# A megakernel's last stage: a new order of its steps

## The chip, the cores and the metric

One core of a Trainium2 chip runs the whole program. The metric is the device time of one execution in microseconds. Three timed runs of the kernel before took 4629.72, 4630.22 and 4632.44 us; the median is 4630.22.

## What is computed

Four layers over 16 images of 128 channels and 32 x 32 pixels: attention with 8 heads, a whitening and colouring of the channels, a block with spatial gate, two attentions and a feed-forward part, and last an attention with one head. The changed stage computes what stands here, the end of the third layer and the fourth:

```python
# end of the third layer (its attentions are done; ff_w1's product is what the stage reads)
fused = jax.nn.silu(combined @ ff_w1.T + ff_b1) @ ff_w2.T + ff_b2
final = fused @ out_w.T + out_b
final = group_norm(final.transpose(0, 2, 1).reshape(b, c, h, w), post_g, post_b)
x = final + residual
# fourth layer: C8 = 16, N = 1024 pixels
q = jnp.einsum('oc,bcn->bno', Wq, xf) + bq
k = jnp.einsum('oc,bcn->bon', Wk, xf) + bk[None, :, None]
v = jnp.einsum('oc,bcn->bon', Wv, xf) + bv[None, :, None]
energy = jnp.einsum('bno,bom->bnm', q, k)
attention = jax.nn.softmax(energy, axis=-1)
out = jnp.einsum('bcm,bnm->bcn', v, attention).reshape(B, C, H, W)
return gamma[0] * out + x
```

## The kernel before

The program is a row of stages that follow one another, each with its own semaphores: `attend` for layer one, `statistics`, `whiten`, `gate`, `attend` again, and `closing`, which is the stage at hand. Nothing of `closing` overlaps the stage ahead of it. Its first transfers are issued at 4015 us of the span.

`closing_steps` (L1347) writes the order by hand: each step of each image gets a place on a line on which an image is 8 long and its eight score steps stand at 0.05, 1.05 and so on. The steps are sorted by place, and every engine walks the same sorted list and issues what of each step is its own, in that order, with waits on semaphores ahead of it. So a place says nothing of a time; only the order of an engine's own steps counts. The numbers of buffers come from the same list (`numbered`): each use of a bank waits until the use before it in that bank is read.

The steps of image b, in the order of their data:

- load (SP): both inputs, ff and h, 512 KB each.
- silu: ScalarE a tanh (L1629), VectorE u = (ff + bias) / 2 (L1702) and s = (tanh + 1) * u (L1707).
- w23: a 128 x 128 product in two halves on TensorE (L1563), ScalarE writes fin (L1634).
- stats, group, factors: the group norm. VectorE's statistics (L1053 to L1059), a small product (L1566), VectorE (L1066 to L1072), a power -0.5 on GpSimd (L1513), VectorE g_a and g_b (L1078 to L1083), and ScalarE hb = h + g_b (L1640).
- z: VectorE (L1723), fin * g_a + hb. z is the input of the attention.
- reach, bound, ratio, scales: a bound on the queries and keys, by which they are scaled into half precision (L1729 to L1731, L1569, L1737, L1738, L1516 to L1521, L1743 to L1747).
- qk: two halves of TensorE (L1572), which ScalarE scales (L1648).
- split: GpSimd writes two half-precision parts (L1526, L1528).
- stack (SP): 12 small transfers that put these parts under each other (L1478).
- pair (8 of them): TensorE's scores of 128 queries against 1024 keys (L1584), of which VectorE takes the maxima (L1761).
- lowest, turn: the maxima negated (L1766), transposed by TensorE (L1589), written by VectorE as two half-precision rows (L1771, L1773), and put into the stack by four transfers (L1483).
- score (8 of them, called 0.0 to 0.3 and 1.0 to 1.3 for the two halves of the queries): TensorE's product again, now transposed and with the maxima subtracted (L1596); ScalarE's exponentials (L1658).
- v: values in two halves (L1576), VectorE scales them (L1754).
- pv ("values" below): e times v, four instructions each (L1609), four steps into one bank, and evac: ScalarE's copy of that bank (L1663).
- esum: GpSimd adds the exponentials, three steps a half (L1537, L1540); dsum: TensorE sums them over partitions (L1616), VectorE copies (L1779); sums (SP), recip (VectorE, L1784), invstore and wide (SP): the inverse, spread over all partitions.
- norm: GpSimd osb * inverse (L1544); zb: ScalarE (L1668); final: VectorE's sum (L1790); store (SP, L1501).

TensorE, VectorE, ScalarE, GpSimd and SP thus work on several images at once. Two pairs of banks go round among group, bound, v, pair, turn and dsum: each of these steps needs the bank that the last but one of them used. Three single banks go round among w23, qk and score, and one is left for values. Of the exponentials there are eight buffers, an image's worth.

Of the kernel before, what the change touches and what calls it, by code (L numbers as in the profile page):

```python
# [19 lines left out]
KC = N // P  # L20
# [40 lines left out]
class Heads:  # L61
# [3 lines left out]
    def __init__(self, kind, n, first):  # L65
# [11 lines left out]
                load=-19.4, reach=-15.96, bound=-4.74, qk=(-3.04, -2.27, -0.19, 2.66), v=(1.75, 2.73), proj=(15.99, 17.54)),  # L77
    True: dict(score=0.01, values=0.12, evac=0.13, score2=0.14, rate=(1.79, 1.95, 1.41), lead=(5.35, 4.59, 7.74), lowest=0.17, turn=0.72,
               load=-26.48, reach=-44.42, bound=-21.92, qk=(-20.62, -17.56, 1.31, 1.34), v=(5.02, 12.31), dqk=(0.36, 4.41, 5.28, 9.56),
               dsum=11.93, proj=(25.58, 31.69), first=((-11.0, -3.0), (-3.0, 5.0), (5.0, 12.5), (12.5, 19.5), (19.5, 25.5)))}  # L80
# [1263 lines left out]
                                                   op0=ALU.add, op1=ALU.mult).then_inc(gated_ready, 1)  # L1344


def closing_steps():  # L1347


    at = []  # L1350
    add = lambda time, *step: at.append((time, len(at), step))
    SCORE, VALUES, PIECE, MAXIMA = 0.05, 0.2, 0.5, 0.8
    for b in range(NB):
        start = 8 * b
        add(start - 34, "load", b)
        add(start - 31, "silu", b)
        for half in range(2):
            add(start - 29 + half + PIECE, "w23", b, half)
            add(start - 18 + half + PIECE, "qk", b, half)
            add(start - 5 + half + PIECE, "v", b, half)  # L1360
        add(start - 27.1, "stats", b)
        add(start - 26 + PIECE + 0.01, "group", b)
        add(start - 24.9, "factors", b)
        add(start - 23.8, "z", b)
        add(start - 23, "reach", b)
        add(start - 22 + PIECE + 0.01, "bound", b)
        add(start - 21.4, "ratio", b)
        add(start - 20.0, "scales", b)
        add(start - 16.4, "split", b)
        add(start - 14.5, "stack", b)  # L1370
        for qc in range(KC):
            add(start - 11 + qc + MAXIMA, "pair", b, qc)
        add(start - 3.01, "lowest", b)
        add(start - 3 + MAXIMA + 0.05, "turn", b)
        for i in range(8):
            add(start + i + SCORE, "score", b, i // 4, i % 4)
            add(start + i + 2 + VALUES, "pv", b, i // 4, i % 4)
            if i % 4:
                add(start + i + 0.3, "esum", b, i // 4, i % 4)
        for half in range(2):  # L1380
            add(start + 4 * half + 6, "evac", b, half)
        add(start + 10 + PIECE, "dsum", b)
        add(start + 11, "sums", b)
        add(start + 12.3, "recip", b)
        add(start + 12.4, "invstore", b)
        add(start + 13.3, "wide", b)
        add(start + 14.9, "norm", b)
        add(start + 15.0, "zb", b)
        add(start + 16.1, "final", b)
        add(start + 16.2, "store", b)  # L1390
    return [step for _, _, step in sorted(at)]


def closing(nc, M, V, shared, half_b1, w23, b23, ff_in, h_in, out, scratch):


    zero, ident, ones = (shared[n] for n in ("zero", "ident", "ones"))
    steps = closing_steps()
    st_n = numbered(steps, w23=1, qk=1, score=2)
    mr_n = numbered(steps, group=1, bound=1, v=1, pair=1, turn=1, dsum=1)  # L1400
# [585 lines left out]
```

## Time and profile before

| | |
|---|---|
| median of three timed runs | 4630.22 us |
| the profiled execution's own time | 4632.01 us |
| its span | 4630.2 us |
| mean granted clock of TensorE | 0.955 |
| busy over the whole span: TensorE, VectorE, ScalarE, GpSimd | 89%, 78%, 67%, 33% |
| the last stage, from its first transfer to the end | 4015 to 4630 us |
| busy in one image of its steady part (34.2 us): TensorE, VectorE, ScalarE, GpSimd | 29.9, 26.8, 15.3, 22.8 us |

The page's busy shares are means over stages with different limits, so for this change only the last 615 us are read, image by image. A matmul's busy time is modelled and overlaps the next one's by some 0.07 us; VectorE's and ScalarE's lines overlap their next by about 0.1.

### The profile page before, as it was taken

What the parts mean: (1) busy time and instruction counts of PE and PEld (TensorE: products, weight loads), DVE (VectorE), ACT (ScalarE), POOL (GpSimd) and SP (SyncE); (2) the same over time, 40 slices, a digit from 0 to 9 for tenths busy, and PEclk for the clock granted to TensorE, in tenths of its full rate; (3) what the DMA queues carried; (4) which work ended last, traced back from release to release, by engine and by line L of the source; (5) the groups of instructions that cost most, each with busy time, mean ns of one, the idle gap of its engine ahead of it and who ended that gap; (6) DMA issues with size and microseconds to landing.
All of it is one profiled execution on the core that took longest, in us unless ns stands there. A gap on an engine that the chain in (4) does not pass through costs nothing. (4 is left out here: it accounts for less than half of the span.)

```text
span 4630.2 us, 68670 instructions
## 1 busy us (share of the span) xinstructions
PE 4126.7 (89%) x25550; PEld 1202.0 (26%) x25550; DVE 3594.3 (78%) x4166; ACT 3116.6 (67%) x5561; POOL 1536.1 (33%) x862
## 2 busy tenths in 40 slices
PE   5999999999996775799999999999999999578888
PEld 1222222222221732122222222222222222123333
DVE  7999999999993366788777777788777777278774
ACT  1888888888886454467777777777777777334443
POOL 1111111111110033144433344444433343346666
PEclk6999999999998987899999999999999999779999
DMA  2222322323321254111112212122122210112221
GB/s 62 55 53 63 67 49 65 66 47 67 65 43 45 73 191 139 35 39 46 38 38 49 47 43 50 38 45 49 33 44 50 46 35 18 46 55 73 71 70 53
DMA packets 144281, 261.96 MB, mean 57 GB/s; under 512 B 58192, under 2 KB 58192, under 8 KB 143824
## 3 DMA queue, kind: packets, MB, share of 16 engines
q1 hardware_dynamic: 143952, 257.61, 22.1%
q8 instruction: 201, 3.29, 0.3%
q14 instruction: 128, 1.05, 0.1%
HBM read 155.13 MB, written 85.13 MB: 52 GB/s over the span
## 5 line engine op out<-in xcount | busy, mean ns | idle before, releaser
L703 DVE TENSOR_REDUCE c_mx<-banks 128x2 f32<-128x1024 f32 x1280 | 1525.1, 1220 | 347.4 <-PE banks L496 192.0
L596 ACT ACTIVATE c_e<-banks 128x512 f32<-128x512 f32 x2560 | 1388.4, 595 | 595.7 <-PE banks L530 323.2
L703 DVE TENSOR_REDUCE a_mx<-banks 128x2 f32<-128x1024 f32 x1024 | 1208.9, 1219 | 62.8 <-PE banks L496 53.1
L596 ACT ACTIVATE a_e<-banks 128x512 f32<-128x512 f32 x2048 | 1111.1, 594 | 177.5 <-PE banks L520 155.5
L545 PE MATMUL banks<-a_e,a_vs 128*32 128x512 f32 x4096 | 545.5, 605 | 0.2 <-ACT a_e L596 0.2
L545 PE MATMUL banks<-c_e,c_vs 128*32 128x512 f32 x4096 | 545.5, 605 | 0.0
L441 POOL TENSOR_TENSOR c_esum<-c_e,c_esum 128x1024 f32<-128x1024 f32 x224 | 527.5, 2355 | 36.6 <-ACT c_e L596 11.2
L496 PE MATMUL banks<-a_stack 48*128 48x512 f16 x2048 | 391.4, 391 | 78.4 <-DMA a_stack<-k_halves 25.9
L520 PE MATMUL banks<-a_stack 50*128 50x512 f16 x2048 | 399.4, 387 | 48.2 <-ACT a_e L596 35.1
L520 PE MATMUL banks<-c_stack 50*128 50x512 f16 x2048 | 398.2, 385 | 45.6 <-ACT c_e L596 36.1
L496 PE MATMUL banks<-c_stack 48*128 48x512 f16 x2048 | 377.0, 387 | 23.4 <-DVE c_mx L703 16.9
L438 POOL TENSOR_TENSOR c_esum<-c_e,made 128x1024 f32<-128x1024 f32 x32 | 60.5, 1892 | 689.5 <-ACT c_e L596 689.5
L545 PE MATMUL banks<-c_e,c_vd 128*64 128x512 f32 x1024 | 275.9, 617 | 0.1
L406 POOL TENSOR_TENSOR a_parted<-a_reach,a_over 128x1 f32<-128x1 f32 x16 | 3.1, 191 | 821.8 <-DVE a_reach L685 821.8
L1609 PE MATMUL banks<-d_e,d_vd 128*128 128x512 f32 x512 | 271.2, 655 | 2.6 <-issue 1.9
L520 PEld LDWEIGHTS banks<-c_stack 50*128 50x128 f16 x2048 | 98.7, 93 | 582.8 <-ACT c_e L596 550.0
L520 PEld LDWEIGHTS banks<-a_stack 50*128 50x128 f16 x2048 | 99.3, 93 | 567.1 <-ACT a_e L596 544.3
L1658 ACT ACTIVATE d_e<-banks 128x512 f32<-128x512 f32 x256 | 137.8, 591 | 123.5 <-PE banks L1596 123.0
L526 PE MATMUL banks<-c_dparts 64*128 64x512 f16 x1536 | 208.3, 376 | 1.9 <-ACT c_e L596 1.9
L504 PE MATMUL banks<-c_dparts 64*128 64x512 f16 x1536 | 202.7, 376 | 1.9 <-DVE c_mx L703 1.8
L496 PEld LDWEIGHTS banks<-c_stack 48*128 48x128 f16 x2048 | 96.7, 94 | 408.2 <-DVE c_mx L703 258.1
L496 PEld LDWEIGHTS banks<-a_stack 48*128 48x128 f16 x2048 | 100.2, 94 | 331.5 <-DVE a_mx L703 238.3
(322 smaller groups left out, 4466.1 us busy)
## 6 DMA issues: line engine op xcount, KB each, us to landing
a_stack<-q_halves SPq DMA_DIRECT2D x96, 128.0 KB, 4.3
a_stack<-k_halves SPq DMA_DIRECT2D x96, 128.0 KB, 7.4
c_stack<-q_halves SPq DMA_DIRECT2D x96, 128.0 KB, 4.4
c_stack<-k_halves SPq DMA_DIRECT2D x96, 128.0 KB, 7.5
early_x<-in_x SPq DMA_DIRECT2D x16, 512.0 KB, 9.0
a_res<-in_x SPq DMA_DIRECT2D x16, 512.0 KB, 4.1
q_halves<-a_parts SPq DMA_DIRECT2D x16, 512.0 KB, 2.9
k_halves<-a_parts SPq DMA_DIRECT2D x16, 512.0 KB, 3.8
```

Source lines behind the costliest of these rows:

```text
L406: nc.gpsimd.tensor_tensor(parted[:, 0:n_s], reach[:, 1:1 + n_s], over[:, 0:n_w:3], ALU.mult).then_inc(ratio_step, 1)
L438: nc.gpsimd.tensor_tensor(dst, src, nought, ALU.add).then_inc(esum_done, 1)
L441: nc.gpsimd.tensor_tensor(dst, src, dst, ALU.add).then_inc(esum_done, 1)
L496: mm = nc.tensor.matmul(slot[:, h, :], stack[0][p][rows, two, queries], stack[1][p][rows, two, keys], start=True, stop=True)
L504: mm = nc.tensor.matmul(slot[:, h, :], dparts[0][p][rows, a, queries], dparts[1][p][rows, c, keys], start=(t == 0), stop=(t == 2))
L520: nc.tensor.matmul(bank_of(n - 1 + h), stack[1][p][rows, two, keys], stack[0][p][rows, two, queries], start=True, stop=True).then_inc(st_f ...
L526: nc.tensor.matmul(bank_of(n - 1 + h), dparts[1][p][rows, c, keys], dparts[0][p][rows, a, queries], start=(t == 0), stop=False)
L545: mm = nc.tensor.matmul(po[width * h:width * h + width, :], v, src[:, h, :], start=(kc == 0), stop=(kc == KC - 1), skip_group_check=True, ...
L596: nc.scalar.activation(e[q % 4][:, 2 * i + h, :], bank_of(n - 1 + h), ACT.Exp).then_inc(st_free, 1)
L703: nc.vector.tensor_reduce(mx[j % 2][:, :, i, qc, half], slot[:, :, :], AX.X, ALU.max).then_inc(mr_free, 1)
L1609: mm = nc.tensor.matmul(po, vd[p][:, kc, :], e[block_of(b, half, kp) % 8][:, c, :], start=(kc == 0), stop=(kc == KC - 1), skip_group_check ...
L1658: nc.scalar.activation(e[q % 8][:, c, :], bank_of(n - 1 + c), ACT.Exp).then_inc(st_free, 1)
```

## The change

`closing_steps` is rewritten; no other function is touched. Every kind of step has a place of its own in two tables, relative to its image's start. Steps that stand in a loop over i = 0 to 7 (score, values, esum, pair) have an offset each. No instruction, wait or buffer is written differently; only the sorted list differs, and with it the numbering of the banks.

```diff
@@ -1344,50 +1344,32 @@
                                                    op0=ALU.add, op1=ALU.mult).then_inc(gated_ready, 1)
 
 
+CLOSING = {
+    "load": -40.2, "silu": -36.43, "stats": -30.68, "group": -26.98, "factors": -25.91, "z": -24.11, "reach": -22.33, "bound": -21.14,
+    "ratio": -20.23, "scales": -19.48, "split": -17.29, "stack": -15.57, "lowest": -3.38, "turn": -2.22, "dsum": 9.93, "sums": 10.43,
+    "recip": 11.73, "invstore": 11.83, "wide": 12.73, "norm": 17.82, "zb": 15.41, "final": 19.03, "store": 19.13}
+CLOSING_HALVES = {"w23": (-34.55, -33.35), "qk": (-18.71, -18.60), "v": (-3.94, -0.43), "evac": (5.66, 9.66)}
+
+
 def closing_steps():
 
 
     at = []
     add = lambda time, *step: at.append((time, len(at), step))
-    SCORE, VALUES, PIECE, MAXIMA = 0.05, 0.2, 0.5, 0.8
+    SCORE, SUMS, VALUES, MAXIMA = 0.01, 1.42, 2.64, -10.54
     for b in range(NB):
         start = 8 * b
-        add(start - 34, "load", b)
-        add(start - 31, "silu", b)
-        for half in range(2):
-            add(start - 29 + half + PIECE, "w23", b, half)
-            add(start - 18 + half + PIECE, "qk", b, half)
-            add(start - 5 + half + PIECE, "v", b, half)
-        add(start - 27.1, "stats", b)
-        add(start - 26 + PIECE + 0.01, "group", b)
-        add(start - 24.9, "factors", b)
-        add(start - 23.8, "z", b)
-        add(start - 23, "reach", b)
-        add(start - 22 + PIECE + 0.01, "bound", b)
-        add(start - 21.4, "ratio", b)
-        add(start - 20.0, "scales", b)
-        add(start - 16.4, "split", b)
-        add(start - 14.5, "stack", b)
-        for qc in range(KC):
-            add(start - 11 + qc + MAXIMA, "pair", b, qc)
-        add(start - 3.01, "lowest", b)
-        add(start - 3 + MAXIMA + 0.05, "turn", b)
+        for kind, when in CLOSING.items():
+            add(start + when, kind, b)
+        for kind, places in CLOSING_HALVES.items():
+            for half in range(2):
+                add(start + places[half], kind, b, half)
         for i in range(8):
+            add(start + i + MAXIMA, "pair", b, i)
             add(start + i + SCORE, "score", b, i // 4, i % 4)
-            add(start + i + 2 + VALUES, "pv", b, i // 4, i % 4)
+            add(start + i + VALUES, "pv", b, i // 4, i % 4)
             if i % 4:
-                add(start + i + 0.3, "esum", b, i // 4, i % 4)
-        for half in range(2):
-            add(start + 4 * half + 6, "evac", b, half)
-        add(start + 10 + PIECE, "dsum", b)
-        add(start + 11, "sums", b)
-        add(start + 12.3, "recip", b)
-        add(start + 12.4, "invstore", b)
-        add(start + 13.3, "wide", b)
-        add(start + 14.9, "norm", b)
-        add(start + 15.0, "zb", b)
-        add(start + 16.1, "final", b)
-        add(start + 16.2, "store", b)
+                add(start + i + SUMS, "esum", b, i // 4, i % 4)
     return [step for _, _, step in sorted(at)]
```

Per engine, the list of one image in the middle of the stage, before and after ([+1] is a step of the next image, [-1] one of the image before; score s, maxima pair p, values pv):

```
TensorE before: s0.0 pv1.2[-1] p3[+1] s0.1 pv1.3[-1] p4[+1] s0.2 pv0.0 dsum[-1] bound[+3] p5[+1] s0.3 pv0.1 v.0[+1]
  w23.0[+4] p6[+1] s1.0 pv0.2 v.1[+1] w23.1[+4] p7[+1] s1.1 pv0.3 p0[+2] turn[+1] s1.2 pv1.0 qk.0[+3] group[+4]
  p1[+2] s1.3 pv1.1 qk.1[+3] p2[+2]
TensorE after:  s0.0 p3[+1] pv1.2[-1] s0.1 p4[+1] pv1.3[-1] dsum[-1] s0.2 p5[+1] pv0.0 bound[+3] s0.3 p6[+1] pv0.1
  s1.0 v.0[+1] p7[+1] pv0.2 s1.1 group[+4] qk.0[+3] qk.1[+3] w23.0[+5] p0[+2] pv0.3 turn[+1] s1.2 p1[+2] pv1.0
  w23.1[+5] s1.3 p2[+2] v.1[+1] pv1.1
VectorE before: final[-2] z[+3] p3[+1] reach[+3] silu[+4] p4[+1] dsum[-1] bound[+3] p5[+1] v.0[+1] p6[+1] scales[+3]
  recip[-1] v.1[+1] p7[+1] stats[+4] lowest[+1] p0[+2] turn[+1] group[+4] p1[+2] factors[+4] p2[+2]
VectorE after:  p3[+1] stats[+4] p4[+1] reach[+3] dsum[-1] p5[+1] bound[+3] final[-2] p6[+1] silu[+5] recip[-1]
  v.0[+1] p7[+1] scales[+3] lowest[+1] group[+4] p0[+2] turn[+1] factors[+4] p1[+2] p2[+2] v.1[+1] z[+3]
ScalarE before: s0.0 silu[+4] s0.1 evac.1[-1] s0.2 s0.3 w23.0[+4] s1.0 w23.1[+4] s1.1 evac.0 s1.2 qk.0[+3] zb[-1]
  s1.3 factors[+4] qk.1[+3]
ScalarE after:  s0.0 s0.1 evac.1[-1] s0.2 s0.3 silu[+5] s1.0 s1.1 qk.0[+3] qk.1[+3] w23.0[+5] evac.0 s1.2
  factors[+4] w23.1[+5] s1.3 zb[-1]
GpSimd before:  esum0.1 esum0.2 ratio[+3] esum0.3 scales[+3] esum1.1 esum1.2 norm[-1] factors[+4] esum1.3 split[+3]
GpSimd after:   esum1.3[-1] norm[-2] esum0.1 esum0.2 ratio[+3] esum0.3 scales[+3] factors[+4] esum1.1 split[+3] esum1.2
```

## Rows read from the trace of the kernel before

**Rows 1.** Windows over one image: length, busy time of each engine, granted clock.

```profile
4300.93:4335.13 34.20, 29.93 (x102) 10.71 (x101) 26.83 (x37) 15.34 (x25) 22.79 (x14) 0.95 0.23 73
```

**Rows 2.** Timeline, TensorE, one image: start, length, then idle time before and releaser.

```profile
4306.06 0.39 PE L1596 MATMUL banks<-d_stack 50*128 50x512 f16 x2 [2.15 <-ACT d_e L1658]
4306.38 3.18 PE L1609 MATMUL banks<-d_e,d_vd 128*128 128x512 f32 x4
...
4317.49 1.05 PE L1576 MATMUL banks<-mats_sb,d_z 128*128 128x128 f32 x8
...
4318.38 1.02 PE L1563 MATMUL banks<-d_s,w 128*128 128x512 f32 x2
4319.34 0.39 PE L1584 MATMUL banks<-d_stack 48*128 48x512 f16 x2
...
4319.88 1.98 PE L1609 MATMUL banks<-d_e,d_vd 128*128 128x512 f32 x4
4321.70 1.05 PE L1576 MATMUL banks<-mats_sb,d_z 128*128 128x128 f32 x8
...
4328.03 0.30 PE L1589 MATMUL banks<-mats_sb,d_negm 128*128 128x128 f32 x1 [1.65 <-DVE d_negm L1766]
```

**Rows 3.** Timeline, ScalarE, around the first of these waits.

```profile
4303.71 1.15 ACT L1640 ACTIVATE d_hb<-d_h,d_g_b 128x1024 f32<-128x1024 f32 x1 [3.45 <-DVE d_g_b L1083]
...
4305.43 1.06 ACT L1658 ACTIVATE d_e<-banks 128x512 f32<-128x512 f32 x2
```

**Rows 4.** Timeline, VectorE and GpSimd, the same time.

```profile
4300.93 2.30 DVE L1078 TENSOR_TENSOR d_g_a<-d_g_rstd,vecs_sb 128x1 f32<-128x1 f32 x1 [1.42 <-POOL d_g_rstd L1513]
...
4305.86 2.91 DVE L1723 SCALAR_TENSOR_TENSOR d_z<-d_fin,d_g_a,d_hb 128x1024 f32<-128x1024 f32 x1
...
4300.86 2.36 POOL L1540 TENSOR_TENSOR d_esum<-d_esum,d_e 128x1024 f32<-128x1024 f32 x1
4305.60 2.09 POOL L1526 TENSOR_TENSOR d_parts<-d_qkf,made 64x1024 f16<-64x1024 f32 x1 [2.39 <-ACT d_qkf L1648]
```

**Rows 5.** By tile, whole stage: count, least, median and greatest duration in ns.

```profile
L1723 DVE SCALAR_TENSOR_TENSOR d_z<-d_fin,d_g_a,d_hb x16: 1275/2914/2918, 4035.7 to 4511.8; 128x1024 f32<-128x1024 f32 x16
...
L1078 DVE TENSOR_TENSOR d_g_a<-d_g_rstd,vecs_sb x16: 150/2296/2300, 4033.9 to 4506.8; 128x1 f32<-128x1 f32 x16
...
L1744 DVE SCALAR_TENSOR_TENSOR d_factor<-d_over,d_balance x16: 127/1393/1851, 4041.6 to 4526.7; 32x1 f32<-32x1 f32 x16
...
L1059 DVE SCALAR_TENSOR_TENSOR d_g_pair<-d_g_pair x16: 219/1026/1030, 4031.6 to 4498.5; 128x1 f32<-128x1 f32 x16
...
L1731 DVE SCALAR_TENSOR_TENSOR d_wr<-d_largest,d_xm,d_nothing x16: 220/222/3966, 4038.3 to 4517.0; 128x2 f32<-128x2 f32 x16
...
L1702 DVE TENSOR_SCALAR d_u<-d_ff,vecs_sb x16: 742/748/755, 4023.3 to 4482.6; 128x1024 f32<-128x1024 f32 x16
...
L1761 DVE TENSOR_REDUCE d_mx<-banks x128: 1206/1218/1226, 4066.2 to 4580.3; 128x2 f32<-128x1024 f32 x128
...
L1528 POOL TENSOR_TENSOR d_parts<-d_qkf,d_parts x16: 2116/2985/2990, 4053.6 to 4542.8; 64x1024 f16<-64x1024 f32 x16
```

**Rows 6.** Timeline, VectorE and GpSimd, at g_a and g_b of an earlier image.

```profile
4131.51 0.15 DVE L1078 TENSOR_TENSOR d_g_a<-d_g_rstd,vecs_sb 128x1 f32<-128x1 f32 x1
4131.69 2.19 DVE L1080 SCALAR_TENSOR_TENSOR d_g_b<-d_g_group,d_g_a,vecs_sb 128x1 f32<-128x1 f32 x1
...
4131.50 2.37 POOL L1540 TENSOR_TENSOR d_esum<-d_esum,d_e 128x1024 f32<-128x1024 f32 x1 [0.47 <-ACT d_e L1658]
```

**Rows 7.** Timeline, TensorE: the first pair, score 0.0 of images 0, 12, 13, the end.

```profile
4065.58 0.61 PE L1584 MATMUL banks<-d_stack 48*128 48x512 f16 x2 [4.39 <-DMA d_stack<-d_parts]
...
4096.71 0.61 PE L1596 MATMUL banks<-d_stack 50*128 50x512 f16 x2 [0.23 <-DMA d_stack<-d_low]
...
4507.21 0.38 PE L1596 MATMUL banks<-d_stack 50*128 50x512 f16 x2
...
4538.19 0.38 PE L1596 MATMUL banks<-d_stack 50*128 50x512 f16 x2
...
4613.06 1.48 PE L1616 MATMUL banks<-d_esum,mats_sb 128*32 128x512 f32 x6 [1.95 <-POOL d_esum L1540]
```

## The prediction

> **What bounds the kernel now.** I read the windows over whole images first, then each engine's timeline over one image, and last the spread of single instructions. In the steady part of the changed stage an image takes 34.2 us, with TensorE busy 29.9, VectorE 26.8, GpSimd 22.8 and ScalarE 15.3 us, at a granted clock of 0.95 [rows 1]; five such windows differ by 0.03. No engine is full, so the order decides: every engine walks one list, and a step that waits holds all that stands behind it.
>
> TensorE's timeline shows two waits in an image: 2.15 us ahead of score 0.1 at 4306.06, until ScalarE's exponentials are done, and 1.65 at the turn, until VectorE has negated the maxima [rows 2]. Behind the first the clock is at 1.2 GHz and not 2.4: the four values instructions take 3.18 instead of 1.98, and with the pairs around them some 1.6 us are lost. Some 0.5 us more go in short waits for banks. What is left, 34.2 - 2.15 - 1.65 - 1.6 - 0.5 = 28.3 us, I take as 28.2: TensorE's own work. From start to start a v step takes 0.89, w23 0.96, pair and score together 0.54, a values step 1.82 ahead of v and about 1.9 elsewhere [rows 2].
>
> The first wait goes back through ScalarE and VectorE: the exponentials at 4305.43 stand behind hb, which waited 3.45 for g_b [rows 3], and g_a ahead of that took 2.30 us for 128 elements, because GpSimd's esum ran from 4300.86 to 4303.22 [rows 4]. That is the pattern on which the forecast rests. z takes 1.28 at least and 2.91 in the median, g_a 0.15 and 2.30, factor 0.13 and 1.39; and the other way round GpSimd's second split 2.12 and 2.99 [rows 5]. z at 4305.86 starts under GpSimd's 4305.60 instruction [rows 4]. So a VectorE instruction with two SBUF tensors and a GpSimd one exclude each other. The maxima, from PSUM, stay within 1.21 to 1.23 in all 128 cases [rows 5]. At 4131.5 one sees who is next: g_a is let through, then GpSimd's waiting instruction, and g_b, 0.2 us later, takes 2.19 [rows 6].
>
> **What the change does.** No instruction and no transfer is added or removed; only the lists differ. silu, stats and w23 run one image farther ahead; group stands right behind score 1.1, ahead of both qk, and these stand together ahead of w23; values i stands behind the pair that follows score i+2; the turn stands behind values 0.3, not right behind pair 0; v.1 goes to the end of the image; esum comes 1.1 places later; norm and final go three places back; dsum and recip come 0.6 earlier. On SP's queue the stack transfers stay ahead of sums, store goes between sums and invstore, load runs an image farther ahead. In my walk the stack lands 14 us before its first pair and the inverse an image before norm, so SP's moves cost nothing; if that cover were gone, pair 0 or norm would be seen waiting for a DMA.
>
> The two old waits go: the pow of factors no longer stands behind norm on GpSimd, hb no longer stands just ahead of the exponentials of 0.0, stats no longer holds the negated maxima, and 1.9 us of values cover the turn. What is late next is in the walk.
>
> **The walk through one image.** Zero is the start of score 1.1; v.0 ends on VectorE at 1.4, and the walk must come back to that. Durations are those of [rows 4, 5]: esum and norm 2.35, splits 2.1 each, s and y about 1.22, pair 1.22 less the tenth by which the next overlaps it; small ones (scales 0.45, lowest 0.1, group 0.6, pow 0.55, dsum copy 0.6) are summed in the same way.
> 1. VectorE: pair 7, scales, lowest, group end at 3.6. TensorE's group needs v.0's bank and waits until 1.4: 1.05 lost.
> 2. GpSimd: pow to 4.2, esum 1.1 to 6.5, first split to 8.6.
> 3. VectorE's turn ends at 7.7. g_a finds the first split running and ends at 8.75; the second split is next, until 10.9; g_b ends at 11.1, pair 1 at 12.4.
> 4. TensorE is at v.1 at 11.0, but v.1 needs the bank that pair 1 frees: start 12.45, 1.45 lost. This wait is new; queued behind it are values 1.1 and the next image's scores, for which ScalarE waits.
> 5. TensorE ends dsum at 12.45 + 0.9 + 1.9 + 2 x 2.45 + 1.9 = 22.1. esum 0.1 waits for that and runs to 24.5.
> 6. VectorE comes to wr at 22.7, behind z (which esum 1.3 held until 16.55), pair 3, stats, pair 4 and the reduction of z. It waits until 24.5; the dsum copy ends at 25.3. TensorE's bound could start at 24.45: 0.9 lost.
> 7. pair 5 to 26.45 (0.4 lost at pair 6); final, held by esum 0.2, to 28.2; pair 6 to 29.3; u to 30.05; s, held by esum 0.3 until 31.3, to 32.5; recip and v.0 to 33.35.
> 8. TensorE: from bound at 25.35 it is 6.6 us to the next score 1.1, at 31.95. v.0 ended 1.4 after it: the walk closes.
> The period is 28.2 + 1.05 + 1.45 + 0.9 + 0.4 = 32.0 us. VectorE has about 21 us of own work (26.8 less what today's g_a, z, factor and stats lose) and in the walk some 8.5 us of waits for GpSimd: that is where part of the gain stays. ScalarE has room: exponential 1.3 ends at 14.2, ahead of score 0.0 at 15.2. No wait is as long as 2.15, so I take the clock at 2.4 GHz; the bounds for it are 0 and the 1.6 us of now.
>
> **Where rule and row pull apart.** u has one SBUF tensor and a constant; its 16 cases took 0.742 to 0.755 us [rows 5], and none of them began under a GpSimd instruction. In step 7 it does. No row prices that: the bounds are 0 and the rest of an esum, here 0.75 for the period, since s waits behind it anyway. I take 0, as for the maxima, and keep 0.75 for a rival. The Trainium skill, SBUF — State Buffer, "SBUF: two separate sides", has a pair of ports under an exclusive lock, held for a whole instruction by GpSimd, by a VectorE instruction with two SBUF inputs, or by one in a two-port fast mode. The rows of g_a and z agree with its first part; if u is in such a mode, the rule speaks for the longer period.
>
> **The sum.** The profiled run has a span of 4630.2 and a time of 4632.0; the median of the three timed runs, 4630.2, is 1.8 below that.
> - Images 0 to 11: score 0.0 begins at 4096.71 for image 0 and 4507.21 for image 12, 34.2 each [rows 7]. At 32.0: 12 x 2.2 = -26.
> - Start: the first pair waited for the stack at 4065.58 [rows 7]. qk0.1 now stands ahead of group 1, so the first split, and the stack with it, can start some 2 us earlier. From that pair to the first score it took 31.1 us [rows 7]; the new list between them has, by the same durations, 20 us of VectorE's work up to turn 0 and some 4 of waits, and some 5 for the maxima's transfers: 29 to 30. Together -3, bounds 0 and -8.
> - Image 12, with fewer leading steps, took 31.0 (4538.19 less 4507.21): -1. The rest is near TensorE's own work already.
> - End: dsum 15 waited 1.95 for the last esum [rows 7], which stood behind norm 14. Norm 14 now stands behind it: -2.
> Together -32: 4632.0 - 32 = 4600.0, and as a median 4598.
>
> **Rivals.**
> - TensorE bound: the phases fall so that g_b and wr slip through, as wr does now (median 0.222 [rows 5]). The period is 28.2 + 1.0, another 12 x 2.8 = 34 less: 4564. Against it: GpSimd's 22.8 us lie in some 30, more densely than now.
> - u waits too: period 32.75, +9: 4607. This is the skill's rule at work.
> - The moves are hidden, since the new waits bring the slow clock back: 32.0 + 1.6 and a share of u: period 33.9, +23: 4621, not to be told from no change.
> - Slower: two more VectorE instructions of the ring, the last one of stats (L1059) and the first factor (L1744), meet a whole GpSimd instruction each: 2 x 2.3 on the way to v.0. Period 36.6, +55: 4653. It decides from a period of 35.5 on. For it: both meet one now (1.03 and 1.39 in the median [rows 5]). Against it: in the walk GpSimd is idle or just starting when these two come.
>
> **Chances.** Forecast 0.35, u waits 0.15, TensorE bound 0.25, hidden 0.14, slower 0.11. A measurement tells about 0.2% (9 us) from no change: faster is below 4621, slower above 4639.5. The hidden case lies half on either side of the first line and the slower one partly below the second: faster 0.80, same 0.11, slower 0.09. The range takes in the forecast, u, most of the TensorE-bound case and the lower half of the hidden one: 4566 to 4622.
>
> **What would show it.** A window over one image: 32 us, clock 1.00. TensorE no longer waits at score 0.1 and at the turn, but at v.1 (for the maxima) and at the bound (for the dsum copy). On VectorE g_b, wr, z and s are longer than their least time; u at 0.75 or longer settles the open price. dsum 15 follows without a wait. I am wrong in kind if VectorE's busy time per image stays near 26.8 us (then the period is 29 to 30), if the clock still drops once an image, or if the first score comes later than 4096.7.

## The result, and the profile after

| | before | after |
|---|---|---|
| median of 8 runs each | 4632.56 us (4629.72 to 4640.19) | 4620.73 us (4616.80 to 4626.87) |
| span of the profiled run | 4630.2 us | 4617.3 us |
| steady image of the changed stage | 34.2 us | 34.04 us, some 35.6 to 36.7 |
| busy in such an image: TensorE, VectorE, GpSimd | 29.9, 26.8, 22.8 us | 28.6, 30.9, 23.7 us |

The ratio is 0.9974, 95% interval 0.9965 to 0.9982: faster by about 12 us, where I had forecast 32. The time lies inside the range, at its upper end, but by luck, as the next table shows.

The stage's own marks, in the two profiled runs, say where 12.9 us of span came from:

| stretch | before | after | difference | forecast |
|---|---|---|---|---|
| start of the stage (earlier stages, not the change) | 4015.12 | 4012.36 | -2.8 | 0 |
| stage start to score 0.0 of image 0 | 81.6 | 77.8 | -3.8 | -3 |
| images 0 to 11 | 410.5 | 412.0 | +1.5 | -26 |
| image 12 | 31.0 | 26.9 | -4.1 | -1 |
| image 13 | 25.3 | 23.8 | -1.5 | 0 |
| image 14 | 23.4 | 23.4 | 0 | 0 |
| score 0.0 of image 15 to the end | 43.3 | 41.1 | -2.3 | -2 |

So the whole shortfall, and more, lies in the twelve steady images, which gained nothing. What was gained lies elsewhere: 2.8 us in stages that the change does not touch, and 4.6 us more than forecast in images 12 and 13. Without those 4.6 the median would be 4625 and outside the range. Windows of three of the twelve (start:end, length, then busy time and instructions of PE, PEld, DVE, ACT, POOL, which are TensorE, its weight loads, VectorE, ScalarE and GpSimd, then granted clock, DMA share, GB/s), to be read against [rows 1]:

```profile
4191.39:4227.23 35.84, 30.04 (x105) 11.84 (x101) 29.69 (x36) 15.58 (x25) 22.57 (x14) 0.95 0.19 68
4295.32:4329.36 34.04, 28.63 (x105) 10.69 (x101) 30.91 (x37) 15.58 (x25) 23.65 (x14) 1.00 0.23 76
4397.44:4434.10 36.66, 31.23 (x103) 12.01 (x101) 31.96 (x37) 15.58 (x25) 26.27 (x15) 0.91 0.25 85
```

At full clock an image takes 34.04 us: next to nothing is gained on 34.2, although TensorE's busy time fell. VectorE issues the same instructions and is busy 4 us longer. In the lines of after, the closing stage's line numbers are 18 lower than in before: L1578 is a score, L1566 a pair, L1591 a values step, L1558 v, L1551 the bound, L1548 the group, L1571 the turn; in the runs below the numbers shift once more. TensorE's timeline of the middle window, against [rows 2]:

```profile
4305.02 0.38 PE L1551 MATMUL banks<-d_wr,mats_sb 128*128 128x2 f32 x2 [0.72 <-DVE d_dsum L1761]
4305.34 0.39 PE L1578 MATMUL banks<-d_stack 50*128 50x512 f16 x2
...
4306.15 0.39 PE L1566 MATMUL banks<-d_stack 48*128 48x512 f16 x2 [0.43 <-DVE d_mx L1743]
...
4313.51 0.38 PE L1548 MATMUL banks<-d_g_pair,mats_sb 128*128 128x2 f32 x2 [1.08 <-DVE d_vd L1736]
...
4318.88 0.27 PE L1571 MATMUL banks<-mats_sb,d_negm 128*128 128x128 f32 x1
...
4326.26 1.16 PE L1558 MATMUL banks<-mats_sb,d_z 128*128 128x128 f32 x8 [3.09 <-DVE d_mx L1743]
```

The waits at score 0.1 and at the turn are gone. The four of the walk are there: bound 0.72 (0.9 forecast), pair 6 0.43 (0.4), group 1.08 (1.05), and v.1, 3.09 where the walk had 1.45. VectorE and GpSimd ahead of that one:

```profile
4319.78 0.61 DVE L1078 TENSOR_TENSOR d_g_a<-d_g_rstd,vecs_sb 128x1 f32<-128x1 f32 x1
4320.43 4.46 DVE L1080 SCALAR_TENSOR_TENSOR d_g_b<-d_g_group,d_g_a,vecs_sb 128x1 f32<-128x1 f32 x1
4324.92 0.15 DVE L1083 TENSOR_SCALAR d_g_b<-d_g_b 128x1 f32<-128x1 f32 x1
4324.99 2.35 DVE L1743 TENSOR_REDUCE d_mx<-banks 128x2 f32<-128x1024 f32 x2
```

```profile
4318.49 1.89 POOL L1508 TENSOR_TENSOR d_parts<-d_qkf,made 64x1024 f16<-64x1024 f32 x1
4320.45 2.12 POOL L1510 TENSOR_TENSOR d_parts<-d_qkf,d_parts 64x1024 f16<-64x1024 f32 x1
4322.54 2.33 POOL L1522 TENSOR_TENSOR d_esum<-d_esum,d_e 128x1024 f32<-128x1024 f32 x1
```

g_b comes as the second split begins, as in the walk. But it ends at 4324.89, with the end of esum 1.2 (4324.87), not with that of the split (4322.57): GpSimd's next instruction, which follows without a gap, goes ahead of it too. 128 elements take 4.46 us.

In all four images of over 35 us (of the twelve) the clock falls around this same wait. Two short windows (length, PE busy and instructions, granted clock, DMA share, GB/s), the first inside the wait ahead of v.1 and the second at v.1, in the image of 36.66, then TensorE's lines:

```profile
4425.00:4427.00 2.00, 0.29 (x4) 1.00 0.01 1
...
4428.00:4430.00 2.00, 1.61 (x7) 0.50 0.27 55
```

```profile
4428.39 2.07 PE L1558 MATMUL banks<-mats_sb,d_z 128*128 128x128 f32 x8 [3.10 <-DVE d_mx L1743]
4430.26 3.62 PE L1591 MATMUL banks<-d_e,d_vd 128*128 128x512 f32 x4
```

v takes 2.07 for 1.16 (so too at 4185.68, 4222.59 and 4465.13) and its values step 3.62 for some 1.9: 2.6 us. In the middle window above the same wait, 3.09, leaves the clock at 2.4 GHz. The longer images (36.66, 35.84, 36.66 and 35.57) add 8.6 us to the twelve. The image behind the first two of them, from 4227.23 to 4261.28, is 34.05 long only by coincidence: its mean clock is 0.95, g_b takes 2.27 and v.1 waits 1.45, as in the walk, but the group waits 1.76 and pair 6 0.84. So a period alone doesn't say which waits made it.

What the other lines of the forecast look like, by instruction (least, median, largest ns), against [rows 5]:

```profile
L1080 DVE SCALAR_TENSOR_TENSOR d_g_b<-d_g_group,d_g_a,vecs_sb x16: 219/4456/4464, 4032.5 to 4491.9; 128x1 f32<-128x1 f32 x16
...
L1684 DVE TENSOR_SCALAR d_u<-d_ff,vecs_sb x16: 742/2478/2492, 4020.5 to 4447.8; 128x1024 f32<-128x1024 f32 x16
...
L1705 DVE SCALAR_TENSOR_TENSOR d_z<-d_fin,d_g_a,d_hb x16: 1276/2638/3131, 4034.9 to 4499.7; 128x1024 f32<-128x1024 f32 x16
```

u, 0.742 to 0.755 in all cases of before, takes 2.48 when it begins just behind the start of an esum. s, which the walk had held by that esum, takes 1.22 to 1.23 in all 16 images: u has taken the wait from it. wr takes 1.84 to 1.86 in the steady images that begin at full clock, as in the walk, and 0.22 in the four that begin behind a slow v.1.

### The profile page after: what moved, and what is told of

Read it like the earlier page. It is cut to its first block and busy times, and to the rows that moved or that the text cites. A ratio compares the mean times of both kernels' runs of the same rounds, so it can differ in the third digit from the quotient of the medians.

```text
span 4617.3 us, 68670 instructions
## 1 busy us (share of the span) xinstructions
PE 4119.0 (89%) x25550; PEld 1205.5 (26%) x25550; DVE 3623.1 (78%) x4166; ACT 3119.1 (68%) x5561; POOL 1543.9 (33%) x862
## 3 DMA queue, kind: packets, MB, share of 16 engines
q14 instruction: 128, 1.05, 0.1%
## 5 line engine op out<-in xcount | busy, mean ns | idle before, releaser
L496 PE MATMUL banks<-c_stack 48*128 48x512 f16 x2048 | 377.4, 387 | 22.8 <-DVE c_mx L703 16.4
L1591 PE MATMUL banks<-d_e,d_vd 128*128 128x512 f32 x512 | 263.0, 638 | 2.0 <-ACT d_osb L1645 0.7
L1743 DVE TENSOR_REDUCE d_mx<-banks 128x2 f32<-128x1024 f32 x128 | 154.4, 1216 | 45.9 <-PE banks L1566 45.8
```

The source lines that it names most:

```text
L496: mm = nc.tensor.matmul(slot[:, h, :], stack[0][p][rows, two, queries], stack[1][p][rows, two, keys], start=True, stop=True)
L1591: mm = nc.tensor.matmul(po, vd[p][:, kc, :], e[block_of(b, half, kp) % 8][:, c, :], start=(kc == 0), stop=(kc == KC - 1), skip_group_check ...
L1743: nc.vector.tensor_reduce(mx[p][:, qc, :], slot[:, :, :], AX.X, ALU.max).then_inc(mr_free, 1)
```

## The experiments

Two theories stood at the start. Theory 1: the shortfall is g_b's exclusion with GpSimd. Its rival: the whole chain from hb to the exponentials, or TensorE's own work, sets the period, and a shorter g_b only moves the wait. Each kernel is after with the edit shown, if not said otherwise. The comparisons are with before, measured beside each (median 4630.2 to 4632.7).

**g_b with one tensor.** The per-partition constants become scalar operands, so one SBUF tensor is left; the arithmetic is the same.

```
-  g.b = scalar_tensor_tensor(in0=group[:, 0:1], scalar=g.a, in1=g.shift, mult, subtract)
+  g.b = tensor_scalar(group[:, 0:1], g.a, g.shift, mult, subtract)
```

> The kernel after with one instruction per image written otherwise: g_b as an operation on one tensor and two values per partition, not on two SBUF tensors. Same values, same order of steps. In the kernel after, g_b takes 4.46 us in most images (least time 0.22), and TensorE then waits 3.09 us at v.1 for the maxima of pair 1. Theory 1 (the wait for GpSimd is that of a second SBUF tensor, and it sets the period through v.1): g_b falls to about 0.2 us, the wait at v.1 goes, the period falls from 34.0 to 31 or so, 12 images give 35 us: 4585, between 4575 and 4600. Rival (any small VectorE instruction on SBUF waits, constants per partition too): g_b stays at 4.46, the time at 4620. Rival (TensorE's banks and VectorE's total set the period anyway, the wait moves on): g_b short, but the period falls by less than 1 us: above 4608.

Measured 4572.13, ratio 0.9877 [0.9861, 0.9894]: 58.7 us under the before of its session; after is 11.8 under its own, so this is 47 us better than after. A window, VectorE at g_a and g_b, TensorE at v.1:

```profile
4272.56:4303.45 30.89, 28.57 (x103) 10.69 (x103) 26.76 (x37) 15.70 (x25) 23.67 (x14) 1.00 0.25 83
```

```profile
4297.32 0.61 DVE L1379 TENSOR_TENSOR d_g_a<-d_g_rstd,vecs_sb 128x1 f32<-128x1 f32 x1
4297.96 0.28 DVE L1381 TENSOR_SCALAR d_g_b<-d_g_group,d_g_a,vecs_sb 128x1 f32<-128x1 f32 x1
4298.27 0.15 DVE L1383 TENSOR_SCALAR d_g_b<-d_g_b 128x1 f32<-128x1 f32 x1
...
4300.64 1.16 PE L1568 MATMUL banks<-mats_sb,d_z 128*128 128x128 f32 x8
```

g_b begins as close to the second split (GpSimd, 4297.98) as in after, and takes 0.28; the one-tensor negation behind it, 0.15, runs under the split. v.1 is without a wait, and the period is 34.04 less the 3.09: 30.9. The clock is 1.00 from 4100 to 4500. Theory 1 holds, a little beyond its own range: one instruction on 128 elements was worth 47 us. Twelve periods shortened by 3.15 are 38 of it, and the low clock's 8.6, which the theory had left out, are most of the rest.

**g_a as well.** `g.a = tensor_scalar(rstd, gain, None, mult)`.

> As the first, with g_a in one-tensor form too (it takes 0.61 us in the kernel after, 0.15 at least). Theory 1: another 0.46 us per image at most, and it counts only if v.1 still waits: 0 to 5 us below the first. If g_b was held only because g_a had let GpSimd's second split through first, then this one differs from the first by nothing in g_b.

4573.46, ratio 0.9882 [0.9866, 0.9899], period 30.88: no more than g_b alone. g_a falls from 0.61 to 0.19, and that was not the cost.

**The same edit in the kernel before.** Is it worth as much in the old order?

> The kernel before, its order kept, with g_a and g_b in one-tensor form. There g_a takes 2.30 us behind esum, hb and the exponentials come behind it, and TensorE waits 2.15 at score 0.1, with half clock after it. Theory 1: g_a falls to 0.15, that wait goes and the clock stays up: 2.15 + 1.6 per image less what comes late next: period 31 to 32, 25 to 40 us less than before: 4590 to 4607. It would then have been one instruction form, and not the order, that held the kernel before. Rival (the wait moves to the turn, which waits 1.65 for a slow instruction of stats): period 33.5 or more, above 4620.

4625.56, ratio 0.9986 [0.9976, 0.9995]: some 5 us, where theory 1 had 25 to 40.

```profile
4334.43 0.21 DVE L1397 TENSOR_SCALAR d_g_a<-d_g_rstd,vecs_sb 128x1 f32<-128x1 f32 x1 [1.41 <-POOL d_g_rstd L1523]
...
4337.52 0.39 PE L1606 MATMUL banks<-d_stack 50*128 50x512 f16 x2
...
4346.26 0.38 PE L1579 MATMUL banks<-d_wr,mats_sb 128*128 128x2 f32 x2 [1.84 <-DVE d_mx L1771]
...
4361.41 0.30 PE L1599 MATMUL banks<-mats_sb,d_negm 128*128 128x128 f32 x1 [1.65 <-DVE d_negm L1776]
```

g_a falls from 2.30 to 0.21 and the 2.15 us at score 0.1 are gone (its line at 4337.52 has no bracket), but the bound now waits 1.84 and the turn still 1.65; the period is 34.08. The rival holds in before, though the wait moved to the bound and not to the turn that it named: the waits are one ring and not separate terms. In the new order the same edit gives 47 us; so the new order made the gain possible and g_b held it back.

**The factors behind pair 1.** If the maxima of pair 1 go ahead of g_a and g_b, v.1's bank comes free early.

```
-  "factors": -25.91 (GpSimd's power, then VectorE's and ScalarE's part)
+  "factors": -25.91 (GpSimd's power alone), "affine": -25.5 (the other two)
```

> The kernel after with one step of VectorE and ScalarE moved: g_a, g_b and hb behind the maxima of pair 1 instead of ahead of them; GpSimd's power stays where it is. g_b may wait as long as it likes now: pair 1 has freed its bank. Theory 1: TensorE's 3.09 us at v.1 go; hb comes no later than 1.2 us later, z with it; period 31.5 to 32.5, so 4590 to 4602. Rival (hb, z and the exponentials behind hb on ScalarE are what is late, not the bank): period as in the kernel after or up to 1.2 us longer, 4620 to 4635.

4597.61, ratio 0.9933 [0.9916, 0.9949], period 32.61.

```profile
4308.16 3.98 DVE L1078 TENSOR_TENSOR d_g_a<-d_g_rstd,vecs_sb 128x1 f32<-128x1 f32 x1
4312.17 0.22 DVE L1080 SCALAR_TENSOR_TENSOR d_g_b<-d_g_group,d_g_a,vecs_sb 128x1 f32<-128x1 f32 x1
...
4310.35 1.16 PE L1558 MATMUL banks<-mats_sb,d_z 128*128 128x128 f32 x8
...
4314.88 0.39 PE L1578 MATMUL banks<-d_stack 50*128 50x512 f16 x2 [1.65 <-ACT d_e L1640]
```

Theory 1's time is met (4590 to 4602), its period by a tenth not: v.1's wait goes. What the rival named appears too, but smaller than it said: score 0.0 now waits 1.65 for exponentials that stand behind hb. And g_a takes over g_b's part, with 3.98 us.

**The splits behind esum 1.2.** `"split": -17.29` becomes `-16.5`.

> The kernel after with one place changed: split at -16.5 instead of -17.29, so GpSimd's list has esum 1.1, esum 1.2, split and no longer esum 1.1, split, esum 1.2. All instructions as they are. In the kernel after, esum 1.1 ends 0.8 us before VectorE has done the turn, and exponential 1.2 is ready 1.5 us after it; so with this order g_a and g_b find GpSimd idle. Theory 1 (the 3.09 us at v.1 are g_b's wait for split and esum): g_a and g_b near their least 0.15 and 0.22, wait at v.1 gone, z may meet a split and take up to 3.3: period 30.9 to 32, 4572 to 4592. It would show that the order alone could have had this gain. Rival (GpSimd is the next to hold things up, since esum 1.3 now comes behind the split and TensorE's dsum waits for it): dsum waits 1 us or more, period above 32.5, 4600 to 4620.

4606.45, ratio 0.9950 [0.9933, 0.9966]. The first three periods are 27.48, 29.83 and 30.88, the fourth is 35.58, then they lock at 34.13.

```profile
4274.15 0.14 DVE L1078 TENSOR_TENSOR d_g_a<-d_g_rstd,vecs_sb 128x1 f32<-128x1 f32 x1
4274.32 0.22 DVE L1080 SCALAR_TENSOR_TENSOR d_g_b<-d_g_group,d_g_a,vecs_sb 128x1 f32<-128x1 f32 x1
4279.41 7.83 DVE L1705 SCALAR_TENSOR_TENSOR d_z<-d_fin,d_g_a,d_hb 128x1024 f32<-128x1024 f32 x1
```

```profile
4279.44 2.12 POOL L1510 TENSOR_TENSOR d_parts<-d_qkf,d_parts 64x1024 f16<-64x1024 f32 x1
4281.52 2.34 POOL L1522 TENSOR_TENSOR d_esum<-d_esum,d_e 128x1024 f32<-128x1024 f32 x1
4283.82 2.33 POOL L1526 TENSOR_TENSOR d_osb<-d_osb,d_wide 128x1024 f32<-128x1024 f32 x1
```

Theory 1's number is missed, though g_a and g_b are down to 0.14 and 0.22: now z waits through three GpSimd instructions in a row, 7.83 us. The rival's 4600 to 4620 is met, and dsum on TensorE waits 3.17 us as it said, but for VectorE's maxima, not for the last esum that it named. So an order alone that frees g_b did not have the gain; another order might.

**The turn right behind pair 0.** `"turn": -2.22` becomes `-2.5`, behind pair 0 as in before.

> The kernel after with one part of the change undone: the turn again right behind pair 0 on TensorE, ahead of values 0.3. In the kernel before it waited 1.65 us there, for the negated maxima; I had said that 1.9 us of values cover it. Cover theory: 0.8 to 1.65 us per image come back, 12 images give 10 to 20 us: 4630 to 4641 (VectorE's turn then comes earlier and g_a and g_b meet other instructions, so this can hide it). Rival (what made the turn wait was stats in VectorE's list, which has gone from there): no wait at the turn in either place, and the time moves only by where g_a then falls: g_a about 1.9 us earlier, under esum 1.1 instead of the split, 4600 to 4625.

4620.89, ratio 0.9982 [0.9973, 0.9992]: that of after, and in the range of this run's rival. The turn waits for nothing (its line at 4281.46 has no bracket), v.1 waits 3.03, g_b takes 4.46.

```profile
4281.14 0.39 PE L1566 MATMUL banks<-d_stack 48*128 48x512 f16 x2
4281.46 0.33 PE L1571 MATMUL banks<-mats_sb,d_negm 128*128 128x128 f32 x1
```

So it is not the values step that took the turn's old 1.65 us away; what is left of my reasons is that stats no longer holds the negated maxima. No run moved stats alone, so this reason stays argued.

**g_b, and u on ScalarE.** Beside the first edit, u leaves VectorE.

```
-  vector: u = tensor_scalar(ff, c_ff_b1, 0.5, add, mult)
+  scalar, behind the tanh: u = activation(ff, Identity, bias=half_b1, scale=0.5)
```

> The first experiment (g_b in one-tensor form) with u computed by ScalarE instead of VectorE, as an identity with scale and bias behind the tanh. In the first one u takes 2.49 us in most images, begun under esum 0.3, 0.75 alone, and TensorE then waits 1.08 at group for v.0's bank. Theory 1: VectorE is 2.4 us earlier at v.0, the wait at group goes, the bound's 0.72 and pair 6's 0.43 stay: period 30.9 - 1.1 = 29.8, 12 x 1.1 = 13 us less than the first: 4556 to 4562. Rival (s takes the wait over, since it has two SBUF tensors and now comes first under esum 0.3; 1.7 us instead): group still waits some tenths, 4563 to 4570. Rival (ScalarE's 1.15 us more hold exponential 1.0): no gain, 4572 or more.

4566.71, ratio 0.9862 [0.9846, 0.9878], period 30.16: 0.7 less than without it. s now stands in u's place under esum 0.3 and takes 2.97, and the group's wait falls from 1.08 to 0.36. That is the rival's 4563 to 4570.

**And wr and g_a with one tensor.** wr becomes two `tensor_scalar` on 128x1.

> As the one before, with g_a and wr in one-tensor form too (wr as two instructions, one per column). wr takes 1.56 us in the first experiment where 0.22 is its least, and the dsum copy behind it makes TensorE's bound wait 0.72, then pair 6 0.43. Theory 1: both go, the period is TensorE's own 28.6 plus a few tenths: 28.6 to 29.2, 4545 to 4556, which would be near what this order can give. Rival (final, held by esum 0.2, keeps VectorE as late): 4556 to 4562.

4560.93, ratio 0.9850 [0.9833, 0.9866], period 30.16.

```profile
4252.96 0.39 PE L1558 MATMUL banks<-d_g_pair,mats_sb 128*128 128x2 f32 x2 [1.03 <-DVE d_vd L1744]
...
4275.54 0.39 PE L1576 MATMUL banks<-d_stack 48*128 48x512 f16 x2 [0.43 <-DVE d_mx L1751]
```

Theory 1's 28.6 to 29.2 is missed. The time falls in the rival's range, but not by what it named: the bound's 0.72 is gone, pair 6's 0.43 stays, and the group's wait has grown back from 0.36 to 1.03. The period didn't move. Where the 5.8 us below the kernel ahead come from is open: the two profiled runs (4562.27 and 4560.17) differ by 2.1, with image 0 shorter by 2.7 (31.85, 29.14) and the earlier stages longer by 2.1.

**esum 1.2 waits for the split.** This tests the one step of my walk that failed. GpSimd's own instruction gets a wait on its own split: no VectorE or TensorE instruction is touched.

```
   pool.wait_ge(st_free, score_n(b, half, kp))
+  if (half, kp) == (1, 2):
+      pool.wait_ge(q_split, min(b + 4, NB))
```

> The kernel after with one wait added on GpSimd: esum 1.2 waits until the second split ahead of it has signalled its end. It comes right behind it anyway, so by itself this costs about the 0.14 us that lie between two esum steps tied in this way. In the kernel after the two follow with no gap, and g_b, held by the second split, is also held by esum 1.2: 4.46 us. My walk had g_b served between the two. Theory A (a small VectorE instruction is let in where GpSimd's next has to wait a moment): g_b takes 2.1 to 2.3 us, the wait at v.1 falls from 3.09 to about 0.8, the period to 31.8, near the 32.0 that I forecast: 4590 to 4600. Theory B (who is next is settled otherwise, esum is served first all the same): g_b 4.5 to 4.7, the time 4620 or up to 2 us more.

4585.55, ratio 0.9896 [0.9879, 0.9912]. The last TensorE line is of a view that ends at 4280, within v.1; the wait in its bracket is whole.

```profile
4275.81 2.16 DVE L1080 SCALAR_TENSOR_TENSOR d_g_b<-d_g_group,d_g_a,vecs_sb 128x1 f32<-128x1 f32 x1
...
4279.35 0.82 PE L1560 MATMUL banks<-mats_sb,d_z 128*128 128x128 f32 x5 [0.79 <-DVE d_mx L1745]
```

```profile
4275.84 2.12 POOL L1510 TENSOR_TENSOR d_parts<-d_qkf,d_parts 64x1024 f16<-64x1024 f32 x1
...
4278.09 2.35 POOL L1524 TENSOR_TENSOR d_esum<-d_esum,d_e 128x1024 f32<-128x1024 f32 x1
```

g_b ends with the split, at 4277.97, and esum starts 0.12 behind it. The period is 31.73, near the walk's 32.0; the waits are 1.07, 0.72, 0.43 and 0.79. Theory A's mechanism holds (g_b 2.16, v.1's wait 0.79, period 31.7); the time is 4.5 us under its range, which had started from 4620 without taking off the low clock's 8.6 us. An added wait makes the kernel 35 us faster, by letting the other engine in.

**The fastest: group behind qk.** The kernel of the g_a, g_b, u and wr edits, and `"group": -26.98` becomes `-26.58`: TensorE does qk before it needs v.0's bank.

> The fastest version so far (g_a, g_b and wr in one-tensor form, u on ScalarE) with group's place at -26.58 instead of -26.98: on TensorE behind both qk, which need nothing of VectorE's banks, instead of ahead of them. In that version TensorE waits 1.03 us at group for v.0's bank in each image of 30.16. Theory 1: 1.0 of it is covered by 2 us of qk, the period is 29.1 to 29.3, 12 images give 11 to 13 us: 4547 to 4552. Rival (VectorE's own list is the bound by now, with 26 to 27 us busy and its waits for GpSimd: group's statistics come 1 us later for VectorE and GpSimd): 4555 to 4562.

4547.02, ratio 0.9814 [0.9797, 0.9830]: 86 us under before and 74 under after.

```profile
4252.93:4281.90 28.97, 28.40 (x102) 10.62 (x101) 25.51 (x37) 16.42 (x26) 23.50 (x14) 1.00 0.26 87
```

Theory 1's time is met. The last long wait is covered: 28.97 us with TensorE busy for 28.4; pair 6's 0.43 is the only wait of over 0.2 us left on it. Only here does TensorE's own work nearly set the period.

**norm and final alone.** Kernel before; norm, final and store three places later (14.9, 16.1, 16.2 become 17.82, 19.03, 19.13), as the change has them.

> The kernel before with one part of the change alone: norm, final and store three places farther back, as in the kernel after. GpSimd's power is then no longer held by norm's 2.35 us. My prediction named that as one of two reasons for the wait of 2.15 us at score 0.1. If the waits were separate terms, the period would fall by 2.15 and by 1.6 of slow clock, to 30.5: 4590. As the run with g_a and g_b in another form has shown the wait moving to the bound (1.84 us there, period 34.08), I expect the like here: period 33 to 34.2, 4615 to 4632. Rival (final and norm now meet other instructions and VectorE is later at the maxima): slower, up to 4645.

4633.01, ratio 1.0003 [0.9993, 1.0012]: no gain, 1 us above the range that I had expected.

```profile
4299.98 0.15 DVE L1078 TENSOR_TENSOR d_g_a<-d_g_rstd,vecs_sb 128x1 f32<-128x1 f32 x1
...
4311.81 0.38 PE L1569 MATMUL banks<-d_wr,mats_sb 128*128 128x2 f32 x2 [0.62 <-DVE d_mx L1761]
...
4320.09 1.16 PE L1576 MATMUL banks<-mats_sb,d_z 128*128 128x128 f32 x8 [0.97 <-DVE d_vd L1754]
```

g_a is free, score 0.1 doesn't wait, and 33.83 us per image is all that this brings: bound, v.1 and the turn (1.67) wait instead, and the last images are slower (29.55 and 28.46 us, before 25.29 and 23.39). Norm's move clears the way to hb and is worth nothing alone. Two images of 32.18 show that the ring can close sooner; why only there stays open.

## Why the prediction was wrong where it was

**Step 3 of the walk failed.** It had g_b held by the second split alone and ending at 11.1, because in [rows 6] a waiting VectorE instruction was served after one GpSimd instruction. It was held by two, for 4.46 us. With the order that the walk assumed, the run in which esum waits for the split, v.1's wait is 0.79 and the period 31.73, against 3.09 and 34.04 in after: that one step is worth 2.3 us per image. That 31.73 is so near the walk's 32.0 is partly luck: the four waits are 3.0 us there against 3.8 in the walk, and what is left for TensorE is 28.7 against 28.2. Against the walk itself, after's 34.04 is 28.7 of TensorE's own and 5.3 in the four waits, where the walk had 28.2 and 3.8; of the 2.04 between them 1.64 is v.1.

**TensorE's own work** was taken 0.5 too low: the period less its four waits is 28.7 in after, and so it is in the run with one-tensor g_b (30.89 less 1.08, 0.72 and 0.43). Over twelve images that is 5 to 6 us.

**The clock.** "No wait is as long as 2.15, so I take the clock at 2.4 GHz" was wrong twice. v.1 waits 3.09, and behind it the clock fell in the four long images, which adds 8.6 us; the mean granted clock is below 1.00 in seven of the twelve images (image 0, these four, and the one behind each pair of them). And a shorter wait is no safeguard: in the run with the factors behind pair 1, whose longest wait in such an image is 1.76, the image from 4215.39 to 4249.65 has a mean clock of 0.90, with a values step of 3.43 us right behind a wait of 1.66. In the run with one-tensor g_b the clock is 1.00 from 4100 to 4500.

**Terms for images 0 to 11** (-26, measured +1.5): twelve times 34.04 would be -2; the first two images (33.54 and 30.74) give 4 more, the last of the twelve (32.75) one, and the low clock takes 8.6 back.

**Start and end** (-3 and -2, measured -3.8 and -2.3) held; dsum 15 follows without a wait:

```profile
4594.54 5.42 PE L1591 MATMUL banks<-d_e,d_vd 128*128 128x512 f32 x12
4599.88 1.91 PE L1598 MATMUL banks<-d_esum,mats_sb 128*32 128x512 f32 x8
```

**Images 12 and 13** (-1 and 0, measured -4.1 and -1.5) were undersized. I called the rest "near TensorE's own work already" and did not split it by waits. This miss of 4.6 us is what brought the time into the range.

**u.** I priced its wait at 0 by the rows of the maxima, and kept 0.75 as a rival. It waits: 2.48 in the median. The Trainium skill, SBUF — State Buffer, "SBUF: two separate sides", has a one-tensor instruction in a two-port fast mode take the same lock. The 2.48 us of u agree with that, if u is in such a mode, which no run shows by itself. Taking u away gives 0.7 us per image, where I had chosen 0. It was the smaller mistake: in after the group's wait still came out at 1.08, for 1.05 in the walk.

**The turn.** Its wait went as forecast, but one of my two reasons (covered by values) fell.

**The rivals.** "Hidden" gave 4621, which is the measured time, by a period of 33.9 from the new waits and a low clock in every image. Measured are 34.04 at full clock from the waits alone and 34.3 in the mean of the twelve. So its number is met partly by luck, with a longer wait for most of what it put down to the clock. I gave it 0.14. "TensorE bound" (period 29.2) needed g_b and wr to slip through by luck; made to do so, with u and group moved too, the kernel gets there (28.97). "Slower" named two other instructions of the ring; g_b was the third of that kind, and its second GpSimd instruction cost 2.3 us, as each of that rival's was priced. Of the signs that I gave against myself, "VectorE's busy time per image stays near 26.8" didn't come: it rose to 30.9, and that is the waits. "The clock still drops once an image" came in part: in seven of the twelve the mean granted clock is 0.76 to 0.95.

## What to carry to other kernels

Look in the trace for the tiny VectorE instructions whose median is many times their least (here 219 ns and 4456), and try the one-tensor form with per-partition scalar operands. It was worth 47 us in the new order and 5 in the old, so it has to be tried in each order. When two engines exclude each other, price the wait of one by a range: from the one instruction that runs to all that are queued behind it, up to that engine's next idle moment or semaphore wait. Both ends were seen here. And when a list is a ring of short waits, count what each edit leaves late next: two edits that each removed the longest wait of before brought 0.1 and 0.4 us per image of 34.2.

## What the hardware showed that I had not expected

- **Who is next is not by turns.** A VectorE instruction that began to wait under the second split (64 partitions, half-precision out), with an esum ready behind it, mostly lost to that as well: over all traces with no gap between the two, g_b in 21 of 21 cases (4.36 to 4.46 us) and g_a in 14 of 16, and z waited 7.83 through three. A z that began to wait under an esum with norm behind it was let in ahead of norm, in 69 of 69 cases over all traces, norm then taking 3.33 to 3.35 instead of 2.35, as here in after. But a d_g_pair instruction on 128x1 in the same position (4149.02, the run with the splits behind esum 1.2) lost to norm and took 3.56. Here is z in after:

```profile
4294.16 3.13 DVE L1705 SCALAR_TENSOR_TENSOR d_z<-d_fin,d_g_a,d_hb 128x1024 f32<-128x1024 f32 x1
```

```profile
4293.85 2.36 POOL L1522 TENSOR_TENSOR d_esum<-d_esum,d_e 128x1024 f32<-128x1024 f32 x1 [3.02 <-ACT d_e L1640]
4296.15 3.35 POOL L1526 TENSOR_TENSOR d_osb<-d_osb,d_wide 128x1024 f32<-128x1024 f32 x1
```

  What decides it (the shape or kind of the running instruction, or of the one that waits, or how the next one is fetched) was not separated and stays open. A semaphore wait between the two GpSimd instructions lets VectorE in.
- **A one-tensor VectorE instruction can wait or not.** u (128x1024, 0.742 to 0.755 alone) takes 2.48 under an esum; g_b as one-tensor on 128x1, with two per-partition scalars, stays at 0.27 to 0.28 in all 16 images, and its negation on 128x1 runs under the split in 0.15. Whether it is the size or the form that spares them no run separated.
- **The clock falls in some waits of 3.1 us and not in others of the same length and place.** Behind waits of 1.65 to 1.67 us it fell in the run with the factors behind pair 1, in three images of twelve, too. What tells them apart no run here shows.
